# A transformer kernel of eleven phases on one core: one GpSimd addition for both rope halves, the high part of split states on ScalarE, and a new order of all four engines

## The chip, the cores and the metric

The kernel runs on one core of a Trainium2 chip. The metric is the device time of one execution in microseconds. Besides the timed runs there is one profiled execution, and every row below is from it. TensorE (PE) multiplies matrices and writes PSUM; VectorE (DVE), ScalarE (ACT) and GpSimd (POOL) work element by element; SyncE (SP) only issues transfers here. Each engine takes its own queue strictly in order, and semaphores tie the queues together.

## The reference

The input is `x` of 16 sequences, 256 tokens and 128 channels. Three sublayers follow each other:

```python
x = x + 0.5 * ffn(layernorm(x))
x = x + attention(layernorm(x))        # 16 heads of 8, causal, softmax
x = x + 0.5 * ffn(layernorm(x))
```

`ffn` is itself a transformer of two layers. A layer shifts half of the channels by one token, multiplies by `wqkv` (128 by 1536), divides the queries and keys of 8 heads of 64 by their length and scales them, applies rotary position factors, and attends over windows of 64 tokens with one window of look-back. It adds the output projection, normalises, and adds a gated MLP (`a * gelu(g)`, 341 hidden columns). The rotation is the part that matters here:

```python
def rotate_half(x):
    x1, x2 = jnp.split(x, 2, axis=-1)
    return jnp.concatenate([-x2, x1], axis=-1)
q = q * cos * scale + rotate_half(q) * sin * scale
```

## The kernel before

**Phases and steps.** Each of the 16 sequences goes through eleven phases (`PHASES`): dense phases 0, 2, 4, 6, 8, 10 and attention phases 1, 3, 7, 9 (local) and 5 (the full one). A phase is a list of steps, tuples of kind, sequence, phase and number, and a step is a list of parts, each on one engine (`PASSES`, `passes`). `("Q", s, ph, n)` is one block of 128 tokens of queries or keys with 512 columns; there are 4 for each sequence in each of the phases 0, 2, 6 and 8, that is 256. Its parts are three products on TensorE (L1702), squares on ScalarE (L1368), the product with the rope table on VectorE, which writes cosine and sine parts side by side (L1617, 128x1024), the sums of squares on VectorE (L1624), and two parts on GpSimd. `rope_join` adds the sine parts to the cosine parts with the halves of each head exchanged, by two instructions (L1228). `rope_scale` bounds the sums (L1235), raises them to the power -1/2 (L1238) and multiplies (L1242). Step `R` then turns the result on TensorE (L1934), and ScalarE copies it (L1386).

**The split.** TensorE multiplies in fp32r, so states are split in a high and a low part. `SPLIT` comes once for each sequence in phases 0, 2, 6 and 8 (64 in all). Both of its instructions run on VectorE: a cast of the state to `h_hi` (L1604), a wait of VectorE for itself, and the subtraction to `h_lo` (L1606). In phases 0 and 6 the state was set by ScalarE (step `STATE`, L1358 and L1359), in phases 2 and 8 by VectorE's addition after `W2` (L1575). The split after a normalisation (`LNT`) has its cast on ScalarE (L1364) and its subtraction on VectorE (L1611) already. Buffers `h_hi` and `h_lo` exist four times; before one is overwritten the engine waits on `bank_filled` for its last reader.

**The order.** Nothing in the code orders the engines by hand. While the kernel is built, `needs` lists what every part waits for, `due_dates` gives each part a due time out of the tables `START_AT`, `STRETCH`, `DUE`, `PHASE_DUE`, `LATER` and `NUDGE`, and `lay_out` plays the work through with the durations of `PASSES` and `passes`, `HANDOVER` between engines and the change of ScalarE's table. On each engine it takes the ready part that is due first, allowing for `PATIENCE`. Out come one in-order list for each of TensorE, ScalarE, VectorE and GpSimd, the buffer that each step uses, and `SERVED`, the order of SyncE's transfers. `tally` counts semaphore values along these lists.

```python
for step, part in POOL_ORDER:
    if (step, part) in POOL_NEEDS:
        pool.wait_ge(sems["prepared"], POOL_NEEDS[step, part])
    take(step, part)
```

## Time and profile before

| what | us |
|---|---|
| timed runs, median of three | 1718.89 |
| timed runs, lowest and highest | 1711.01, 1722.75 |
| the profiled execution | 1712.97 |
| its span (first to last instruction) | 1711.1 |

The span is what the rows divide; the profiled execution's own time is 1.9 us longer, which lies around the span. Busy time of an engine is the time in which it carried out instructions, and its idle time matters only where something later waits for it.

### The profile page before, as it was taken

The numbers are of one execution on the slowest core, as the hardware profiler recorded it, in microseconds if no ns is written. First come the engines' busy times: TensorE is split into PE (matmuls) and PEld (weight loads), VectorE is DVE, ScalarE is ACT, GpSimd is POOL, SyncE is SP. The second block draws the span as 40 slices with busy tenths as digits, with TensorE's granted clock in tenths as the row PEclk, the third lists the DMA queues.
The fourth block names the chain that finished last, engine by engine and source line by source line (L and its number), as shares of the span: only waits on it lengthen the run. The fifth ranks groups of instructions, "written<-read, shape, count | busy, mean of one in ns | idle before, by whom it ended". The sixth has DMA issues, their size and how long they took to land.

```text
span 1711.1 us, 48415 instructions
## 1 busy us (share of the span) xinstructions
PE 1513.9 (88%) x17754; PEld 1229.7 (72%) x17754; DVE 1459.9 (85%) x2978; ACT 1293.4 (76%) x3832; POOL 1310.2 (77%) x1546
## 2 busy tenths in 40 slices
PE   4788889889889999989989899999989899899987
PEld 3667677677767767767777777877766667678776
DVE  8788997888879879989888899988987979888885
ACT  2587768678867888778788877987875687787894
POOL 7899994557857988987889986989831779879890
PEclk9899999889989999999999999999999899999999
DMA  5101112110211101101010030001212002001000
GB/s 140 38 20 26 32 36 59 49 54 21 63 45 29 26 11 53 48 27 55 20 27 20 20 97 25 23 17 45 82 45 97 11 20 63 20 19 24 23 17 14
DMA packets 49635, 66.75 MB, mean 39 GB/s; under 512 B 8146, under 2 KB 32252, under 8 KB 49404
## 3 DMA queue, kind: packets, MB, share of 16 engines
q1 hardware_dynamic: 49404, 63.66, 13.8%
q8 instruction: 146, 2.39, 0.6%
q14 instruction: 85, 0.70, 0.1%
HBM read 22.75 MB, written 15.73 MB: 22 GB/s over the span
## 4 chain that ended last, share of the span: by engine, by line
POOL 31%; DVE 30%; PE 22%; ACT 9%; issue 8%; POOLq 0%; ACTq 0%; DVEq 0%
POOL sums L1238 11%; POOL parts L1228 8%; DVE parts L1617 7%; POOL parts L1242 7%; PE bank L1702 6%; ACT probs L1310 5%; DVE neg_full L1496 4%; DVE sums L1624 3%; DVE neg_max L1496 3%; POOL sums L1235 2%; PE bank L1752 2%; PE bank L1934 2%; PE bank L1889 2%; DVE probs L1526 2%; DVE normal L1563 2%
## 5 line engine op out<-in xcount | busy, mean ns | idle before, releaser
L1228 POOL TENSOR_TENSOR parts<-parts 128x256 f32<-128x256 f32 x512 | 388.7, 785 | 133.8 <-DVE parts L1617 132.5
L1238 POOL TENSOR_TENSOR sums<-sums,neg_half 128x8 f32<-128x8 f32 x256 | 434.8, 1699 | 21.3
L1310 ACT ACTIVATE probs<-bank,neg_max 128x128 f32<-128x128 f32 x1024 | 365.0, 415 | 65.5 <-DVE neg_max L1496 63.7
L1617 DVE TENSOR_TENSOR parts<-bank,rope 128x1024 f32<-128x1024 f32 x256 | 308.5, 1216 | 34.9 <-ACT squares L1368 33.2
L1242 POOL TENSOR_TENSOR parts<-parts,sums 128x512 f32<-128x512 f32 x256 | 282.3, 1103 | 37.9 <-POOL sums L1238 1.7
L1310 ACT ACTIVATION_READ_ACCUMULATOR probs<-bank,neg_max 128x1 f32 x1024 | 259.9, 255 | 0.0
L1934 PE MATMUL bank<-ident,parts 128*128 128x128 f32 x1024 | 165.2, 287 | 56.9 <-POOL parts L1242 50.6
L1368 ACT ACTIVATE squares<-bank 128x512 f32<-128x512 f32 x256 | 157.5, 625 | 52.1 <-PE bank L1702 29.9
L1702 PE MATMUL bank<-wqkv_hi,h_hi 128*128 128x512 f32 x384 | 182.0, 474 | 8.6 <-DVE h_lo L1606 5.0
L1934 PEld LDWEIGHTS bank<-ident,parts 128*128 128x128 f32 x1024 | 120.0, 145 | 91.6 <-issue 65.3
L1526 DVE TENSOR_TENSOR probs<-probs,prob_inv 128x1024 f32<-128x1024 f32 x128 | 174.2, 1361 | 4.4
L1800 PE MATMUL bank<-ident,probs 128*128 128x128 f32 x1024 | 147.6, 288 | 28.0 <-DVE probs L1526 13.2
L1496 DVE TENSOR_REDUCE neg_max<-bank 128x4 f32<-128x512 f32 x256 | 160.0, 680 | 11.6 <-PE bank L1773 10.5
L1624 DVE TENSOR_REDUCE sums<-squares 128x8 f32<-128x512 f32 x256 | 169.3, 674 | 0.2
L1339 ACT ACTIVATE turned<-bank 128x512 f32<-128x512 f32 x256 | 147.5, 652 | 23.6 <-PE bank L1800 23.1
L1800 PEld LDWEIGHTS bank<-ident,probs 128*128 128x128 f32 x1024 | 119.4, 147 | 52.5 <-issue 17.9
L1702 PE MATMUL bank<-wqkv_hi,h_lo 128*128 128x512 f32 x384 | 155.6, 405 | 0.0
L1702 PE MATMUL bank<-wqkv_lo,h_hi 128*128 128x512 f32 x384 | 155.2, 404 | 0.0
L1214 POOL TENSOR_SCALAR var_eps<-mean_var 128x2 f32<-128x2 f32 x112 | 29.7, 265 | 149.4 <-DVE mean_var L1556 144.3
L1773 PE MATMUL bank<-k_t,q_t 64*64 64x128 f32 (+1 forms) x4096 | 138.1, 260 | 0.0
L1496 DVE TENSOR_REDUCE neg_full<-bank 128x2 f32<-128x512 f32 (+1 forms) x192 | 119.7, 683 | 16.9 <-PE bank L1737 10.0
L1773 PEld LDWEIGHTS bank<-k_t,q_t 64*64 64x64 f32 x4096 | 127.5, 135 | 5.4 <-issue 0.6
(147 smaller groups left out, 3821.4 us busy)
## 6 DMA issues: line engine op xcount, KB each, us to landing
between<-val SPq DMA_DIRECT2D x192, 128.0 KB, 2.4
laid_dram<-halves SPq DMA_DIRECT2D x96, 128.0 KB
stacked_q<-laid_dram SPq DMA_DIRECT2D x16, 512.0 KB, 6.3
stacked_k<-laid_dram SPq DMA_DIRECT2D x16, 512.0 KB, 4.1
x_sb<-in_L_attn_x_dram SPq DMA_DIRECT2D x16, 128.0 KB, 2.5
out_dram<-x_sb SPq DMA_DIRECT2D x16, 128.0 KB, 1.8
laid_dram<-plain SPq DMA_DIRECT2D x8, 128.0 KB
raw_qkv<-in_L_ffn_wqkv_dram SPq DMA_DIRECT2D x3, 256.0 KB, 4.2
```

The costliest lines, as they stand in the source:

```text
L1228: last = nc.gpsimd.tensor_tensor(joined[:, :, dst], joined[:, :, dst], sines[:, :, src], ALU.add)
L1238: nc.gpsimd.tensor_tensor(sums[:, u], sums[:, u], neg_half[:], ALU.pow).then_inc(sems["pool_step"], 1)
L1242: nc.gpsimd.tensor_tensor(joined, joined, sums[:, u].rearrange("p (h o) -> p h o", o=1).to_broadcast([P, LOCAL_HEADS, LOCAL_D]), ALU.mult) ...
L1310: last = nc.scalar.activation(probs[:, u, block:block + wide].rearrange("p b j -> p (b j)"), bank[:, at:at + P * wide], ACT.Exp, bias=neg_ ...
L1496: nc.vector.tensor_reduce(dst, src, AX, ALU.max, negate=True).then_inc(sems["max_ready"], 1)
L1526: nc.vector.tensor_tensor(probs[:, u], probs[:, u], prob_inv[:, u].rearrange("p (r o) -> p r o", o=1).to_broadcast([P, BLOCKS, P]), ALU.mu ...
L1617: nc.vector.tensor_tensor(parts[:, u].rearrange("p o (h d) -> p o h d", d=LOCAL_D), bank[:].rearrange("p (o h d) -> p o h d", o=1, d=LOCAL ...
L1624: nc.vector.tensor_reduce(sums[:, ROPE_OF[step]], squares[:, SQUARES_OF[step]].rearrange("p (h d) -> p h d", d=LOCAL_D), AX, ALU.add).then ...
L1702: last = nc.tensor.matmul(dst, lhs, rhs, start=(n == 0), stop=(n == 2))
L1773: last = nc.tensor.matmul(bank[HALF * half:HALF * (half + 1), at + j0:at + P], q_t[a][rows, 2 * n + c, WINDOW * w:WINDOW * (w + 1)], k_t[a ...
L1800: last = nc.tensor.transpose(bank[:, P * n:P * (n + 1)], probs[:, u, block], ident[:])
L1934: last = nc.tensor.transpose(bank[:, P * c:P * (c + 1)], parts[:, u, 0, P * c:P * (c + 1)], ident[:])
```

## The change

`rope_join` becomes one instruction over 128x512. Both operands are seen as heads, halves and 32 columns, and the second one's halves are read in reversed order. The cast of `SPLIT` moves to ScalarE (a new function `split_state`); VectorE waits for it with `high_ready` in place of `vector_step`. The durations with which the order is planned are changed in some places, and the tables of due times (`START_AT` and those after it, here left out) are all new; `NUDGE` has 230 entries in place of 92. With them the order of all engines, the buffers and `SERVED` are new.

```diff
 PASSES = {
-    "SPLIT": [(DVE, 0.87)], "WO": [(PE, 1.65), (DVE, 0.88)],
+    "SPLIT": [(ACTE, 0.27), (DVE, 0.47)], "WO": [(PE, 1.65), (DVE, 0.88)],
...
-    "W1": [(PE, 0.74), (ACTE, 0.36), (DVE, 0.4)], "W2": [(PE, 1.3), (DVE, 1.01)], "OT": [(PE, 0.24), (ACTE, 0.28)], "WOF": [(PE, 0.45), (DVE, 0.36)],
-    "XB": [(POOL, 0.75)], "MT": [(DVE, 0.33), (PE, 0.5), (DVE, 0.6)], "Y": [(ACTE, 0.49)],
+    "W1": [(PE, 0.78), (ACTE, 0.36), (DVE, 0.4)], "W2": [(PE, 1.3), (DVE, 1.01)], "OT": [(PE, 0.24), (ACTE, 0.28)], "WOF": [(PE, 0.45), (DVE, 0.36)],
+    "XB": [(POOL, 0.75)], "MT": [(DVE, 0.45), (PE, 0.45), (DVE, 0.6)], "Y": [(ACTE, 0.49)],
...
-    "Q": [(PE, 0.79), (ACTE, 0.49), (DVE, 1.14), (DVE, 0.6), (POOL, 1.44), (POOL, 3.3)], "R": [(PE, 0.42), (ACTE, 0.49)],
-    "QF": [(PE, 0.85), (ACTE, 0.72), (DVE, 0.79)], "T": [(PE, 0.48), (ACTE, 0.49)]}
+    "Q": [(PE, 0.82), (ACTE, 0.49), (DVE, 1.14), (DVE, 0.6), (POOL, 1.25), (POOL, 3.35)], "R": [(PE, 0.4), (ACTE, 0.49)],
+    "QF": [(PE, 0.85), (ACTE, 0.72), (DVE, 0.79)], "T": [(PE, 0.46), (ACTE, 0.49)]}
...
     if kind in ("S", "E"):
-        return [(PE, 1.23 if not is_full(ph) else (0.88 if n else 1.25) if kind == "S" else (0.7 if n % 3 else 0.97))]
+        return [(PE, 1.1 if not is_full(ph) else (0.74 if n else 1.12) if kind == "S" else (0.7 if n % 3 else 0.97))]
...
     if kind == "N":
-        return [(DVE, 1.42)]
+        return [(DVE, 1.52)]
     if kind == "V":
-        return [(PE, 0.76), (ACTE, 0.28), (PE, 0.24), (DVE, 0.44)] if is_full(ph) else [(PE, 1.07), (ACTE, 0.5)]
+        return [(PE, 0.76), (ACTE, 0.28), (PE, 0.2), (DVE, 0.44)] if is_full(ph) else [(PE, 0.95), (ACTE, 0.5)]
...
-                joined = parts[:, u, 0].rearrange("p (h d) -> p h d", d=LOCAL_D)
-                sines = parts[:, u, 1].rearrange("p (h d) -> p h d", d=LOCAL_D)
-                hd = LOCAL_D // 2
-                for half in range(2):
-
-                    dst, src = slice(hd * half, hd * (half + 1)), slice(hd * (1 - half), hd * (2 - half))
-                    last = nc.gpsimd.tensor_tensor(joined[:, :, dst], joined[:, :, dst], sines[:, :, src], ALU.add)
-                last.then_inc(sems["rope_joined"], 1)
+                joined = parts[:, u, 0].rearrange("p (h o d) -> p h o d", o=2, d=LOCAL_D // 2)
+                sines = parts[:, u, 1].rearrange("p (h o d) -> p h o d", o=2, d=LOCAL_D // 2)
+                nc.gpsimd.tensor_tensor(joined, joined, sines[:, :, ::-1], ALU.add).then_inc(sems["rope_joined"], 1)
...
+            def split_state(step):
+
+                s, before = step[1], SPLIT_BEFORE[step]
+                whole = last_step({"STATE", "W2"}, step)
+                name = "state_set" if whole[0] == "STATE" else "state_ready"
+                act.wait_ge(sems[name], count(name, whole))
+                if before is not None:
+                    act.wait_ge(sems["bank_filled"], later("bank_filled", readers(before)))
+                nc.scalar.activation(h_hi[SPLIT_OF[step]][:], state[s][:, 0:T], ACT.Copy).then_inc(sems["high_ready"], 1)
...
                 elif kind == "SPLIT":
-                    if last_step({"STATE", "W2"}, step)[0] == "STATE":
-                        dve.wait_ge(sems["state_set"], count("state_set", last_step({"STATE"}, step)))
-                    else:
-                        dve.wait_ge(sems["state_ready"], count("state_ready", last_step({"W2"}, step)))
-                    before, h = SPLIT_BEFORE[step], SPLIT_OF[step]
-                    if before is not None:
-                        dve.wait_ge(sems["bank_filled"], later("bank_filled", readers(before)))
-                    nc.vector.tensor_copy(h_hi[h][:], state[s][:, 0:T]).then_inc(sems["vector_step"], 1)
-                    dve.wait_ge(sems["vector_step"], count("vector_step", step))
+                    dve.wait_ge(sems["high_ready"], count("high_ready", step))
+                    h = SPLIT_OF[step]
                     nc.vector.tensor_tensor(h_lo[h][:], state[s][:, 0:T], h_hi[h][:].bitcast(F32),
                                             ALU.subtract).then_inc(sems["split_ready"], 1)
```

## Rows read from the trace of the kernel before

**Rows 1.** The page: span and busy time of each engine (share, instructions):

```profile
span 1711.1 us, 48415 instructions
...
PE 1513.9 (88%) x17754; PEld 1229.7 (72%) x17754; DVE 1459.9 (85%) x2978; ACT 1293.4 (76%) x3832; POOL 1310.2 (77%) x1546
```

**Rows 2.** Windows: length, busy PE, PEld, DVE, ACT, POOL (instructions), clock, DMA share, GB/s:

```profile
100.00:1700.00 1600.00, 1443.62 (x17191) 1173.07 (x17187) 1377.12 (x2791) 1243.35 (x3694) 1229.28 (x1439) 0.97 0.14 37
...
945.00:972.00 27.00, 23.16 (x358) 19.29 (x358) 24.23 (x46) 23.26 (x81) 25.51 (x31) 1.00 0.09 22
```

**Rows 3.** The chain that ended last, whole span: by engine, then by line:

```profile
POOL 31%; DVE 30%; PE 22%; ACT 9%; issue 8%; POOLq 0%; ACTq 0%; DVEq 0%
...
by line: POOL sums L1238 10.6%; POOL parts L1228 8.3%; issue 7.8%; DVE parts L1617 7.2%; POOL parts L1242 6.9%; PE bank L1702 6.0%; ACT probs L1310 4.6%; DVE neg_full L1496 3.6%; DVE sums L1624 3.1%; DVE neg_max L1496 3.0%; POOL sums L1235 
```

**Rows 4.** Waits of TensorE: us, times, longest; last one group of instructions:

```profile
PE bank L1934 <- POOL parts L1242: 50.6, 54, 4.3
...
PE bank L1901 <- DVE normal L1563: 25.3, 17, 11.3
...
PE bank L1800 <- DVE probs L1526: 13.2, 20, 2.5
...
L1737 PEld LDWEIGHTS bank<-mask_full,ident_b 64*64 64x64 bf16 x384 | 7.7, 108 | 12.4 <-DMA stacked_k<-laid_dram 4.0 <-issue 3.9 <-DVE neg_full L1496 0.3
```

**Rows 5.** Groups of instructions: line, form, count, busy us, mean ns, idle before:

```profile
L1228 POOL TENSOR_TENSOR parts<-parts 128x256 f32<-128x256 f32 x512 | 388.7, 785 | 133.8 <-DVE parts L1617 132.5
```

**Rows 6.** One line's instructions: duration ns min/median/max:

```profile
L1228 POOL TENSOR_TENSOR parts<-parts x512: 708/732/1798, 23.4 to 1659.0; 128x256 f32<-128x256 f32 x171
...
L1242 POOL TENSOR_TENSOR parts<-parts,sums x256: 1041/1043/2085, 28.9 to 1665.9; 128x512 f32<-128x512 f32 x128
...
L1235 POOL TENSOR_SCALAR sums<-sums x256: 228/242/1231, 26.3 to 1662.8; 128x8 f32<-128x8 f32 x128
...
L1238 POOL TENSOR_TENSOR sums<-sums,neg_half x256: 1653/1656/2746, 27.1 to 1664.1; 128x8 f32<-128x8 f32 x128
...
L1606 DVE TENSOR_TENSOR h_lo<-state,h_hi x64: 424/426/1156, 18.3 to 1639.5; 128x256 fp32r<-128x256 f32 x64
...
L1611 DVE TENSOR_TENSOR h_lo<-bank,h_hi x80: 391/415/427, 72.7 to 1699.9; 128x256 fp32r<-128x256 f32 x80
```

**Rows 7.** Timeline, 181 to 192 us: start, length; first GpSimd, then VectorE:

```profile
185.25 2.57 POOL L1238 TENSOR_TENSOR sums<-sums,neg_half 128x8 f32<-128x8 f32 x1
...
188.96 2.40 POOL L1228 TENSOR_TENSOR parts<-parts 128x256 f32<-128x256 f32 x2
...
185.06 1.22 DVE L1526 TENSOR_TENSOR probs<-probs,prob_inv 128x1024 f32<-128x1024 f32 x1
...
189.36 1.40 DVE L1526 TENSOR_TENSOR probs<-probs,prob_inv 128x1024 f32<-128x1024 f32 x1
```

**Rows 8.** Groups of the split and of L1526; last two by duration min/median/max:

```profile
L1604 DVE CAST h_hi<-state 128x256 fp32r<-128x256 f32 x64 | 25.8, 403 | 2.3 <-PE bank L1702 1.3 <-ACT state L1359 0.3
...
L1606 DVE TENSOR_TENSOR h_lo<-state,h_hi 128x256 fp32r<-128x256 f32 x64 | 34.4, 538 | 2.2
...
L1526 DVE TENSOR_TENSOR probs<-probs,prob_inv 128x1024 f32<-128x1024 f32 x128 | 174.2, 1361 | 4.4
...
L1524 DVE RECIPROCAL prob_inv<-prob_sum 128x8 f32<-128x8 f32 x128 | 25.2, 197 | 32.5 <-ACT probs L1310 30.8
...
L1364 ACT ACTIVATE h_hi<-bank x80: 367/384/577, 72.2 to 1699.3; 128x256 fp32r<-128x256 f32 x80
...
L1526 DVE TENSOR_TENSOR probs<-probs,prob_inv x128: 1224/1226/2119, 53.0 to 1678.6; 128x1024 f32<-128x1024 f32 x128
```

**Rows 9.** The chain in order of time, 1684 to 1711 us: start, length, what:

```profile
1688.12 0.14 issue
...
1704.60 0.02 issue
```

**Rows 10.** Waits of ScalarE, the longest:

```profile
ACT probs L1310 <- DVE neg_max L1496: 63.7, 43, 3.2
```

More of the change, by code:

```diff
@@ L167 @@
[L167 to L170 removed]
[26 rows of a table removed]
[L197 to L202 removed]
[8 rows of a table removed]
[L211 removed]
[7 rows of a table removed]
+START_AT = (-146.9, -142.3, -458.8, -225.8, 39.3, 17.1, 149.3, 343.7, 1103.2, 1153.0, 855.1, 831.6, 1094.4, 946.4,
+            575.2, 1093.0)
@@ new lines @@
+STRETCH = 2.4717
+PATIENCE = (0.008, 0.0, 0.149, 0.697)
+DUE = {('E', 0, True): 24.6, ('FOLD', 0, False): 357.71, ('FOLD', 1, False): -179.97, ('LNH', 0, False): -125.77,
+       ('LNH', 1, False): -164.34, ('LNH', 2, False): -196.25, ('LNT', 0, False): 97.72, ('LNT', 1, False): 228.36,
+       ('LNT', 2, False): -32.48, ('LNX', 0, False): -99.02, ('LNX', 1, False): 271.99, ('MASKS', 0, False): 170.23,
[5 rows of a table added]
+       False): 2.3, ('SPLIT', 1, False): 16.47, ('STATE', 0, False): 687.9, ('STATE', 1, False): 353.42, ('T', 0,
+       False): -357.05, ('T', 1, False): -55.66, ('V', 0, False): 250.79, ('V', 0, True): -24.65, ('V', 1, False):
+       123.03, ('V', 1, True): 232.55, ('V', 2, True): -555.1, ('V', 3, True): -20.13, ('VAL', 0, False): 274.89,
+       ('VAL', 1, False): 633.81, ('VALF', 0, False): 355.59, ('VALF', 1, False): 857.28, ('W1', 0, False): 107.4,
[4 rows of a table added]
@@ new lines @@
+PHASE_DUE = {0: 192.38, 1: 2.46, 2: 173.79, 3: -404.42, 4: -66.84, 5: -104.61, 6: -5.63, 7: -56.17, 8: 224.03, 9:
+             -235.83, 10: 63.22}
+LATER = {(0, 0): 43.36, (0, 1): 578.39, (0, 2): 242.31, (0, 3): 614.64, (0, 4): 36.82, (0, 5): 285.3, (0, 6): 42.33,
[26 rows of a table added]
+NUDGE = {('E', 4, 5, 3): -8.39, ('E', 5, 5, 2): 2.84, ('E', 5, 5, 3): 1.02, ('E', 5, 5, 4): -6.73, ('E', 5, 5, 5):
+         -10.07, ('E', 6, 5, 2): -15.61, ('E', 8, 5, 0): -582.91, ('E', 8, 5, 3): -33.75, ('E', 12, 5, 1): -130.94,
+         ('E', 13, 5, 1): -52.12, ('E', 13, 5, 3): -142.92, ('E', 14, 5, 2): 7.18, ('E', 15, 5, 1): -66.92, ('E', 15,
+         5, 3): -65.73, ('E', 15, 5, 4): -64.1, ('LNH', 0, 2, 0): -159.5, ('LNH', 1, 2, 0): -203.36, ('LNH', 2, 4, 0):
+         309.01, ('LNH', 2, 8, 0): 486.11, ('LNH', 3, 2, 0): 410.81, ('LNH', 4, 10, 0): 379.39, ('LNH', 6, 10, 0):
+         795.7, ('LNH', 9, 10, 0): -622.56, ('LNH', 11, 4, 0): 386.0, ('LNH', 12, 2, 0): -675.3, ('LNH', 14, 4, 0):
+         551.52, ('LNT', 2, 10, 0): 252.15, ('LNT', 3, 4, 1): 455.1, ('LNT', 4, 2, 0): 283.63, ('LNT', 4, 4, 0):
+         19.05, ('LNT', 5, 2, 0): -430.37, ('LNT', 7, 8, 0): 230.96, ('LNT', 8, 4, 0): -429.31, ('LNT', 13, 2, 0):
+         -84.82, ('LNT', 13, 10, 0): 343.78, ('LNT', 14, 4, 1): 938.07, ('LNT', 15, 4, 0): 410.18, ('LNX', 3, 0, 0):
+         165.56, ('LNX', 10, 0, 0): -1127.88, ('LNX', 12, 0, 0): 6.57, ('LNX', 15, 0, 0): -264.71, ('MT', 3, 5, 0):
[22 rows of a table added]
+         -40.41, ('SPLIT', 6, 8, 0): -326.47, ('SPLIT', 10, 8, 0): 856.81, ('SPLIT', 13, 6, 0): -67.59, ('SPLIT', 14,
[6 rows of a table added]
+         9, 1): -223.99, ('VAL', 0, 8, 0): -105.47, ('VAL', 3, 8, 1): -345.91, ('VAL', 12, 2, 0): -194.96, ('VAL', 12,
+         2, 1): -198.42, ('VAL', 13, 0, 0): 253.78, ('VAL', 13, 0, 1): 248.62, ('VALF', 13, 4, 0): -402.87, ('W1', 1,
[14 rows of a table added]
@@ L838, in emits @@
         "STATE": [{}, {"state_set": 1}],
-        "SPLIT": [{"vector_step": 1, "split_ready": 1}],
+        "SPLIT": [{"high_ready": 1}, {"split_ready": 1}],
         "Q": [{}, {"squares_ready": 1}, {"rope_parts": 1}, {"squares_summed": 1}, {"rope_joined": 1},
@@ L1408, in _ @@
                     copy_heads(step)
+                elif step[0] == "SPLIT":
+                    split_state(step)
                 else:
```

17 lines of the change are left out of this document (removed), and 131 rows, old and new, of tables (DUE, LATER, NUDGE).

## The prediction

> **What bounds the kernel now.** I read the engine totals first. The span is 1711.1 us, and TensorE, VectorE, GpSimd and ScalarE are busy for 88, 85, 77 and 76% of it [rows 1]. No engine is full, and none is idle enough to be forgotten. Next comes the table by stretch. In the 1600 us between the start and the last steps TensorE is busy for 1443.6 us, so it idles for 156.4 us; where rope work lies thick (945 to 972 us) GpSimd is busy for 25.51 of 27 us [rows 2]. What a better order can win in the middle is therefore less than 156.4 us in the best case, since matmuls are neither added nor removed.
>
> Third is the chain that ended last. It runs 31% through GpSimd, 30% through VectorE, 22% through TensorE and 9% through ScalarE, and the join of the rope halves alone (L1228) is 8.3% of it [rows 3]. That is a list of engines taking turns, not one bottleneck. Last come the waits of TensorE. The largest is for the scaled rope parts, 50.6 us in 54 waits; those for VectorE (normal 25.3, probs 13.2) follow. Transfers hardly count: a TensorE weight load waited 4.0 us for one, so the new order of SyncE's queue (values shifted, halves written and spread, results stored) I price at nothing as long as that stays so [rows 4].
>
> **Part A, one join instead of two.** Removed are 512 GpSimd additions of 128x256 with a mean of 785 ns, or 1.57 us for each of 256 pairs [rows 5]; added are 256 additions of 128x512 in which the second operand's halves are read in reversed order. No row of before has that operation. From below: the 128x512 product with a broadcast operand, shortest 1.04 us. From above: the pair itself, 1.57 us, no gain; a loss I exclude from this term, since the same elements go in the same runs of 32 with one start fewer. Between these, a line through two undisturbed sizes: the 128x256 addition takes 0.73 us, and a one-operand 128x8 operation 0.24 us, which I take as the fixed part. So 256 columns cost 0.49 us and 512 columns 0.24 + 0.98 = 1.22 us [rows 6]. This is a plain addition with two full operands, so it lies nearer to this line than to the broadcast product.
>
> The means lie above the undisturbed times because GpSimd and VectorE get in each other's way. Two GpSimd additions from 188.96 us took 2.40 us instead of 1.43 while the VectorE product of two SBUF tensors (L1526) ran from 189.36 us. A power from 185.25 us took 2.57 us (its shortest is 1.653) beside the same product, begun at 185.06 us [rows 6, 7]. The pair carries 1.57 - 1.43 = 0.14 us of this. One start in place of two I let carry a bit over half, 0.09 us. The join then costs 1.22 + 0.09 = 1.31 us and saves 0.26 us, 66 us of GpSimd over 256. The new table of durations in the diff lowers its own entry for the join from 1.44 to 1.25, that is by 0.19 us, or 49 us over 256, which is the same size; I take 0.24 us, 61 us in all. On the chain stand 0.083 x 1711.1 = 142 us of L1228, or 142 / 1.57 = 90 pairs [rows 3, 5]; they give 90 x 0.24 = **22 us**. The bounds: nothing, and with the broadcast product's 1.04 plus 0.09 us, 90 x 0.44 = 40 us.
>
> **Part B, the cast on ScalarE.** 64 VectorE casts with a mean of 403 ns (25.8 us) go [rows 8]. VectorE has 0.30 x 1711 = 513 us of chain for 1460 us of work, 0.35 us for each us, so this gives 25.8 x 0.35 = 9 us [rows 1, 3]. ScalarE gets 64 copies of 128x256. Its copy of that size and type out of PSUM has a median of 384 ns [rows 8], so 24.6 us, and at 0.09 x 1711 / 1293 = 0.12 they cost 3 us. The same 0.38 us stands for a source in SBUF, for which there is no row of this form. Half of the splits (32) follow a VectorE addition to the state and so get a new crossing to ScalarE and back; crossings take 0.02 to 0.14 us on the chain [rows 9], which makes at most 32 x 0.28 = 9 us, times 0.35 some 2 us at middle values. Sum: **a gain of 4 us**. What hides the cast is ScalarE's own idle time. The new wait stands in ScalarE's in-order queue: behind it queue the exponentials, the copies of turned probabilities and the gelus, for which TensorE and VectorE wait. ScalarE's waits for row maxima are 63.7 us in 43, 1.48 us each [rows 10]. If every cast stopped it as long, 64 x 1.48 = 95 us at 0.12 would cost 11 us. Bounds of B: a gain of 9 us, a loss of 11 us.
>
> **Part C, the longer hold.** VectorE's subtraction of two SBUF tensors (L1606) has a shortest time of 424 ns and a longest of 1156: the difference of 732 ns is the length of one GpSimd addition. The same subtraction with one operand in PSUM (L1611) never took over 427 ns [rows 6, 8]. A longer GpSimd instruction so makes the two-SBUF operations wait longer. L1526 stands 135 ns above its shortest in the mean (1361 against 1226 in the median) and L1606 114 ns (538 - 424), in all 128 x 0.135 + 64 x 0.114 = 24.6 us [rows 8]. If all of it grew as 1.22 / 0.73, it would be 17 us more, 6 us on the chain. Only the waits behind joins grow, so I take **2 us lost**; bounds 0 and 6.
> By the Trainium skill (SBUF — State Buffer, section on the two separate sides) whichever of GpSimd and a VectorE instruction in a two-port mode or with two SBUF inputs begins first keeps the pair of ports for its whole instruction. The trace agrees for L1606 and L1526. By that rule one 1.22 us hold costs an operation that falls into it at random more than two of 0.73 us do (1.22 x 1.22 / 2 = 0.74 against 0.53 us squared), and a cast moved off VectorE ends one such clash; it would leave the sum as it is, since both stand in A to C.
>
> **Part D, the order laid out anew.** Nothing is computed that was not before; all four queues are sorted by other due times. The durations it plans with move by up to 0.14 us (a score unit 1.23 to 1.10, a weighted sum 1.07 to 0.95, the scaling of probabilities 1.42 to 1.52; the trace has 0.197 + 1.361 = 1.56 us for the last, so 1.52 is nearer [rows 8]). Without a new order I would count only half of A and B, because waits that ran beside the chain move onto it; that the order is made for the shorter steps is my reason for counting them whole. Beyond that, TensorE's two waits for VectorE above come to 38.5 us; I take some 15% of them, **6 us** [rows 4]. The bounds are wide: a third of the 156.4 us idle (52 us) won, or as much lost as the rope wait costs now (50.6 us).
>
> **The sum.** 22 + 4 - 2 + 6 = 30 us, from the profiled execution's 1712.97 us: 1683 us. The median of the three timed runs, 1718.89, is 5.9 us higher and their scatter is 11.7 us; I add half of that difference: **1686 us**, 1.9% below the median. Its own range is 1668 to 1702 us. The granted TensorE clock in the middle is 0.97 in the mean (the level of 2.4 GHz with short falls to 1.2) [rows 2]; I leave it there.
>
> **The rivals.**
> *Hidden* (0.20): the rope work is faster, but the chain's other strands, just as full, take its place, and the saved GpSimd time becomes GpSimd idle time. For: four engines within 12 points of one another. Against: 50.6 us of TensorE's waits are exactly for this work. Time: half of A and nothing else, 1719 - 11 = 1708 us, from 1702 to 1719.
> *Deeper* (0.14): the new order also fills a third of TensorE's idle 156.4 us. For: nothing in the rows forces these gaps to be there. Against: VectorE at 85% is itself close. Time: 1686 + 6 - 52 = 1640 at the far end, 1655 us as a middle.
> *The join costs what the pair cost* (0.05): GpSimd handles the reversed 4-dimensional pattern slower, and A is nought. Time: 1686 + 22 = 1708 us. For: no such pattern in the trace; against: the diff's 1.25 us.
> *Slower* (0.08): the new order brings TensorE's turning of the rope parts (L1934) nearer behind their scaling on GpSimd than before, and all that is queued behind it waits. Now this takes 50.6 us in 54 of 256 turnings. If twice as many wait, that is 50.6 us more against 30 won, 1719 + 20 = 1739 us. It decides from 50.6 + 30 = 81 us of such waits on. For: a plan made with mean durations leaves in-order queues no room for the 2.57 us powers. Against: the old order was of the same kind, and GpSimd now ends sooner.
>
> **Chances.** Forecast 0.53, hidden 0.20, deeper 0.14, join dear 0.05, slower 0.08. A measurement of this kernel can tell about 1% from no change, so 1701.7 us is the border for faster. Faster by over 1%: 0.53 + 0.14 = 0.67; within 1%: 0.20 + 0.05 = 0.25; slower by over 1%: 0.08. The range goes down to 1652 us, past the middle of the deeper case, and up to 1716 us, over most of the hidden one.
>
> **What will show each step.** A: 256 GpSimd instructions in place of 512, mean between 1.2 and 1.4 us, GpSimd busy near 1249 us. B: no VectorE cast of 128x256 but those of the weights, 64 more ScalarE copies of 0.38 us, VectorE near 1434 us busy, ScalarE near 1318. C: L1606's successor and L1526 with longest times of up to 1.22 us above their shortest, means up by no more than 0.1 us. D: TensorE's wait for the scaled rope parts below 40 us, and its idle middle near 130 us. Wrong would be: a join mean at or above 1.57 us; that wait above 81 us; waits of ScalarE for the state in tens of microseconds; or GpSimd's idle time grown by as much as its work fell, at an unchanged span.

## The result, and the profile after

| | before | after |
|---|---|---|
| median, us | 1714.93 (20 runs) | 1724.68 (20 runs) |
| lowest, highest | 1706.75, 1724.42 | 1714.97, 1734.62 |
| span of the profiled execution | 1711.1 | 1718.5 |

The ratio after to before is 1.0052, 95% interval 1.0034 to 1.007: a small loss of some 9 us where 1.9% of gain was forecast. 1686 us was wrong, and the time also lies above the range (1652 to 1716 us).

The page of after, engine totals, and below them the chain that ended last, by engine and by line:

```profile
span 1718.5 us, 48157 instructions
...
PE 1511.3 (88%) x17754; PEld 1223.7 (71%) x17754; DVE 1445.8 (84%) x2914; ACT 1325.7 (77%) x3904; POOL 1276.6 (74%) x1290
...
POOL 31%; PE 24%; DVE 21%; ACT 11%; issue 7%; DMA 4%; SPq 2%; POOLq 0%; ACTq 0%; DVEq 0%
```

Against [rows 1]: GpSimd is busy for 33.6 us less and VectorE for 14.1 us less. Yet GpSimd's idle time went from 1711.1 - 1310.2 = 400.9 to 1718.5 - 1276.6 = 441.9 us. The work went, and the engine waits instead. The chain holds as much of GpSimd as before (31%) [rows 3], and has 4% of DMA and 2% of SyncE's queue, which it did not have.

The windows of after, columns as in [rows 2]:

```profile
100.00:1700.00 1600.00, 1435.86 (x17076) 1162.86 (x17075) 1355.94 (x2715) 1269.66 (x3737) 1189.57 (x1188) 0.97 0.13 37
```

TensorE idles for 164.1 us in the middle where it idled for 156.4.

The changed operations of after, groups by line (busy us, mean ns, idle before), with the table loads of ScalarE:

```profile
L1257 POOL TENSOR_TENSOR parts<-parts 128x512 f32<-128x512 f32 x256 | 342.2, 1344 | 132.6 <-DVE parts L1650 131.7
...
L1566 DVE TENSOR_TENSOR probs<-probs,prob_inv 128x1024 f32<-128x1024 f32 x128 | 178.1, 1391 | 4.4
...
L1639 DVE TENSOR_TENSOR h_lo<-state,h_hi 128x256 fp32r<-128x256 f32 x64 | 39.4, 616 | 9.6 <-ACT h_hi L1389 9.3
...
L1389 ACT ACTIVATE h_hi<-state 128x256 fp32r<-128x256 f32 x64 | 27.5, 429 | 15.7 <-PE bank L1735 8.0 <-DVE state L1615 6.7
...
L1433 ACT ACT_TABLE_LOAD x48 | 61.6, 1283 | 0.9
...
L1338 ACT ACT_TABLE_LOAD x36 | 46.2, 1283 | 0.6
```

The join has its forecast size: 1.344 us, against 1.31. VectorE's products of two SBUF tensors got dearer in the mean: the scaling of probabilities 1391 ns after 1361, the subtraction 616 after 538 [rows 8]. ScalarE did the casts in 27.5 us; the last two groups and the 12 other loads make 96 table loads where before had these two:

```profile
L1395 ACT ACT_TABLE_LOAD x44 | 56.5, 1283 | 3.1 <-PE bank L1702 2.3
...
L1310 ACT ACT_TABLE_LOAD x31 | 39.8, 1283 | 0.6
```

and 13 others, 88 in all. The new order costs 8 x 1.283 = 10.3 us of ScalarE in table changes.

Waits of TensorE in after (us, times, longest):

```profile
PE bank L1967 <- POOL parts L1270: 56.9, 62, 4.2
PE bank L1934 <- DVE normal L1603: 23.2, 18, 11.3
...
PE bank L1833 <- DVE probs L1566: 19.4, 22, 3.2
```

Against [rows 4]: the wait for scaled rope parts grew from 50.6 to 56.9 us though GpSimd has less to do, the wait for scaled probabilities from 13.2 to 19.4 us, and a new one stands beside them, for the transfers of the full phase (the weight load's own wait, 4.0 us before):

```profile
PEld bank L1770 <- DMA stacked_k<-laid_dram: 11.8, 4, 5.4
...
PE bank L1770 <- DMA stacked_k<-laid_dram: 10.8, 4, 5.3
```

One place of the timeline of after shows what the engines do to each other (start, length):

```profile
708.27 1.28 POOL L1257 TENSOR_TENSOR parts<-parts 128x512 f32<-128x512 f32 x1 [0.61 <-DVE parts L1650]
...
708.34 2.30 DVE L1566 TENSOR_TENSOR probs<-probs,prob_inv 128x1024 f32<-128x1024 f32 x1
...
1264.08 1.23 DVE L1566 TENSOR_TENSOR probs<-probs,prob_inv 128x1024 f32<-128x1024 f32 x1
1264.12 2.32 POOL L1257 TENSOR_TENSOR parts<-parts 128x512 f32<-128x512 f32 x1
```

At 708 us the join began 0.07 us before the product; the join took its undisturbed 1.28 us and the product 2.30 instead of 1.22. At 1264 us the product began 0.04 us before the join; now the product is whole and the join takes 2.32 instead of 1.28. Which engine loses a little over 1 us (1.08 or 1.04) is decided by hundredths of a microsecond, and neither the order of before nor that of after looks at it. Below, *clash* means this.

### The profile page after: what moved, and what is told of

The parts are those of the page before. It is cut to its first block, busy times and chain, and to the rows that moved or that the text cites. A ratio compares the mean times of both kernels' runs of the same rounds, so it can differ in the third digit from the quotient of the medians.

```text
span 1718.5 us, 48157 instructions
## 1 busy us (share of the span) xinstructions
PE 1511.3 (88%) x17754; PEld 1223.7 (71%) x17754; DVE 1445.8 (84%) x2914; ACT 1325.7 (77%) x3904; POOL 1276.6 (74%) x1290
## 4 chain that ended last, share of the span: by engine, by line
POOL 31%; PE 24%; DVE 21%; ACT 11%; issue 7%; DMA 4%; SPq 2%; POOLq 0%; ACTq 0%; DVEq 0%
POOL sums L1266 11%; POOL parts L1270 7%; POOL parts L1257 7%; PE bank L1735 6%; DVE parts L1650 5%; ACT probs L1338 4%; DMA laid_dram<-halves 3%; DVE neg_full L1536 3%; POOL sums L1263 2%; PE bank L1967 2%; PE bank L1922 2%; PE bank L1833 2%; DVE sums L1657 2%; POOL rstd L1249 2%; PE bank L1785 2%
## 5 line engine op out<-in xcount | busy, mean ns | idle before, releaser
L1266 POOL TENSOR_TENSOR sums<-sums,neg_half 128x8 f32<-128x8 f32 x256 | 438.2, 1712 | 21.3
L1257 POOL TENSOR_TENSOR parts<-parts 128x512 f32<-128x512 f32 x256 | 342.2, 1344 | 132.6 <-DVE parts L1650 131.7
L1967 PE MATMUL bank<-ident,parts 128*128 128x128 f32 x1024 | 164.0, 284 | 64.5 <-POOL parts L1270 56.9
L1566 DVE TENSOR_TENSOR probs<-probs,prob_inv 128x1024 f32<-128x1024 f32 x128 | 178.1, 1391 | 4.4
L1833 PE MATMUL bank<-ident,probs 128*128 128x128 f32 x1024 | 152.0, 291 | 31.7 <-DVE probs L1566 19.4
L1247 POOL TENSOR_SCALAR var_eps<-mean_var 128x2 f32<-128x2 f32 x112 | 33.8, 302 | 172.9 <-DVE mean_var L1596 167.4
L1922 PE MATMUL bank<-q_t,wo 128*128 128x256 f32 x512 | 125.7, 389 | 9.8 <-ACT q_t L1378 6.0
```

What stands on the lines that cost most here:

```text
L1257: nc.gpsimd.tensor_tensor(joined, joined, sines[:, :, ::-1], ALU.add).then_inc(sems["rope_joined"], 1)
L1266: nc.gpsimd.tensor_tensor(sums[:, u], sums[:, u], neg_half[:], ALU.pow).then_inc(sems["pool_step"], 1)
L1566: nc.vector.tensor_tensor(probs[:, u], probs[:, u], prob_inv[:, u].rearrange("p (r o) -> p r o", o=1).to_broadcast([P, BLOCKS, P]), ALU.mu ...
L1833: last = nc.tensor.transpose(bank[:, P * n:P * (n + 1)], probs[:, u, block], ident[:])
L1922: last = nc.tensor.matmul(bank[:, 0:T], w[:, c], o[:, c], start=(c == 0), stop=(c == CHUNKS - 1))
L1967: last = nc.tensor.transpose(bank[:, P * c:P * (c + 1)], parts[:, u, 0, P * c:P * (c + 1)], ident[:])
```

## The experiments

Every ratio is to runs of before, which were repeated beside each batch of kernels on the same chip; the table gathers them.

| run | operations | order of the queues | ratio | 95% |
|---|---|---|---|---|
| after | both edits | after's | 1.0052 | 1.0034 to 1.007 |
| old_join | join | before's | 0.9992 | 0.9973 to 1.001 |
| old_cast | cast | before's | 1.0011 | 0.9995 to 1.0028 |
| old_both | both edits | before's | 1.0008 | 0.9989 to 1.0026 |
| new_two | cast | after's | 1.0165 | 1.0143 to 1.0187 |
| new_dve | join | after's | 1.0157 | 1.0136 to 1.0178 |
| new_none | neither | after's | 1.0174 | 1.0149 to 1.0198 |
| old_spread | neither, no wait for laid halves | before's | 0.9991 | 0.9977 to 1.0005 |
| new_spread | both, no wait for laid halves | after's | 1.004 | 1.0025 to 1.0055 |
| after_exclusive | both edits | after's, moved with the exclusion | 0.9715 | 0.9693 to 0.9737 |
| after_ignorant | both edits | after's, moved without it | 0.9909 | 0.9886 to 0.9932 |
| before_exclusive | neither | before's, moved with it | 0.9737 | 0.9715 to 0.976 |
| both_exclusive | both edits | before's, moved with it | 0.9601 | 0.9578 to 0.9624 |
| both_ex_two | cast | that of both_exclusive | 0.9784 | 0.9732 to 0.9835 |
| sh_before_1 | neither | before's, 300 blind moves | 1.0047 | 1.002 to 1.0073 |
| sh_before_2 | neither | before's, 300 others | 1.0068 | 1.0042 to 1.0094 |
| sh_after_1 | both edits | after's, 300 blind moves | 1.0081 | 1.0059 to 1.0104 |

**The edits in the order of before.** Three kernels of before: with the one addition, with the cast on ScalarE (put into its queue where the plan has the state ready; after's `split_state` and `high_ready`), and with both.

```diff
-                for half in range(2):
...
-                    last = nc.gpsimd.tensor_tensor(joined[:, :, dst], joined[:, :, dst], sines[:, :, src], ALU.add)
-                last.then_inc(sems["rope_joined"], 1)
+                nc.gpsimd.tensor_tensor(joined, joined, sines[:, :, ::-1], ALU.add).then_inc(sems["rope_joined"], 1)
```

```diff
+        at = [n for n, y in enumerate(queue) if (y in DONE_AT and y[0][0] != "SPLIT" and
+                                                 DONE_AT[y] - passes(y[0])[y[1]][1] >= ready)][0]
+        queue.insert(at, (x, 0))
```

Expected of old_join:

> The kernel of before with its order, buffers and due times untouched; only the two GpSimd additions of rope_join become one. Theory G (the edits gain, the new order gives it back): the chain holds 90 pairs, each now shorter by 1.57 - 1.34 = 0.23 us, so up to 21 us less than before; with parallel strands taking over half, 10 us; ratio 0.988 to 0.994. Theory H (the edits are hidden behind other strands): within 3 us of before, ratio 0.998 to 1.002, and GpSimd's idle time grows by what its work loses, some 50 us.

Expected of old_cast:

> The order of before; only the cast of each split state moves to ScalarE, put into its queue at the time at which the plan of before has the state ready. Theory G: 4 us faster (9 us off VectorE's share of the chain, 5 us back on ScalarE and for crossings), ratio 0.995 to 1. Theory H: nothing, ratio 0.999 to 1.002. Theory L (the cast costs on ScalarE, because the in-order queue stops there for the state): 5 to 11 us slower, ratio 1.003 to 1.006, with ScalarE waits for the state above 30 us.

Expected of old_both:

> The order of before with both edits. Theory G: the sum of the two single runs, 14 to 25 us faster than before, ratio 0.985 to 0.992; the new order would then have to cost 24 to 35 us. Theory H: ratio 0.998 to 1.002, and the new order costs the 9 us that after is slower.

Measured: 0.9992, 1.0011, 1.0008. In a fixed order the edits are worth nothing that can be told from no change, together or alone. The engine totals of old_join, its scaling of probabilities, and two waits of TensorE:

```profile
span 1711.8 us, 48159 instructions
...
PE 1509.6 (88%) x17754; PEld 1225.0 (72%) x17754; DVE 1472.9 (86%) x2978; ACT 1294.7 (76%) x3832; POOL 1270.5 (74%) x1290
```

```profile
L1521 DVE TENSOR_TENSOR probs<-probs,prob_inv 128x1024 f32<-128x1024 f32 x128 | 180.5, 1410 | 4.4
```

```profile
PE bank L1929 <- POOL parts L1237: 41.9, 43, 3.6
...
PE bank L1795 <- DVE probs L1521: 23.1, 31, 3.6
```

GpSimd is busy for 39.7 us less and idle for 40.4 us more, at an unchanged span: what the prediction gave as the mark of a hidden gain. The waits show where it went. TensorE's wait for rope parts fell by 8.7 us (50.6 to 41.9), and its wait for scaled probabilities rose by 9.9 us (13.2 to 23.1) [rows 4]. A product that falls behind a join can now be held by an instruction of 1.28 us and not of 0.73; its mean rose from 1361 to 1410 ns [rows 8], and VectorE is busy for 13.0 us more. So the gain was not only hidden, it was handed from one pair of engines to the other. The trace of old_both has the same trade (42.6 and 21.7 us of the two waits); that the two sums cancel at the end of the chain is read from the unchanged time and was not tested apart.

**The edits undone in the order of after.** Three kernels of after: with two additions per join, with the cast on VectorE, with both undone.

```diff
                 elif step[0] == "SPLIT":
-                    split_state(step)
+                    pass
...
-                    dve.wait_ge(sems["high_ready"], count("high_ready", step))
...
+                    nc.vector.tensor_copy(h_hi[h][:], state[s][:, 0:T]).then_inc(sems["vector_step"], 1)
+                    dve.wait_ge(sems["vector_step"], count("vector_step", step))
```

Expected of new_none:

> The order and the due times of after, but with two GpSimd additions for each join and the cast on VectorE directly ahead of its subtraction: the new order alone. Theory G: the order costs 24 to 35 us on top of undone edits worth 14 to 25 us less: 1.015 to 1.025 of before. Theory H: 9 us slower than before like after itself, ratio 1.003 to 1.008. Either way TensorE waits for the spread transfers of the full phase should show as in after, some 22 us of matmuls and weight loads, where before had 4.

Expected of new_two:

> After with two GpSimd additions for each join; its order and the cast on ScalarE stay. The new order without both edits stood at 1.0174 of before, after itself at 1.0052, so the edits together are worth 1.2% there. If the join carries it (theory P: the new order leaves the rope work on GpSimd no room): ratio 1.013 to 1.017. If the cast carries it (theory Q): 1.005 to 1.009. If both alike: 1.011.

Expected of new_dve:

> After with the cast on VectorE directly ahead of its subtraction; one addition for the join. Theory P: ratio 1.005 to 1.008, the cast is worth little. Theory Q: 1.013 to 1.017. If both alike: 1.011.

Measured: 1.0174, 1.0165, 1.0157. Undoing the join costs 1.1% (1.0165 against 1.0052), undoing the cast 1.05%, and both together 1.2%, not their sum. The same edits were worth nothing in the order of before. They have no price of their own, then. The departures are not alike: shorter work put into the order of before changed nothing, the old and longer work put back into the order of after cost about 1%, whichever part of it came back. The reading is that an order loses when a step outlasts the time that it was planned with and wins nothing when a step ends early; these six kernels fit it, and no run tests it apart. The 1.0174 of new_none lies where theory G had it, though old_both (1.0008 against 0.985 to 0.992) had refuted G; and of the theories for new_two and new_dve none had each edit costing as much as both. TensorE's wait for rope parts in new_two:

```profile
PE bank L1972 <- POOL parts L1275: 85.0, 83, 4.2
```

That is 28.1 us above after's 56.9, of which 18.5 us reach the median (1743.17 against 1724.68).

**The new wait for transfers.** Can the loss of after be its four waits for the full phase's stacked keys? In both orders the rearranged halves were loaded from a constant tensor and not from the one that the halves are written to, directly behind the writes, so that SyncE waits for no write ahead of them. The full phases then compute with the constants of that tensor in place of the halves.

```diff
-                    sp.wait_ge(written[u][w], WRITES * nth)
...
-                                 laid[u, w].rearrange("j b (d c) t -> (j b d) (c t)", c=CHUNKS)).then_inc(spread[u], 16)
+                                 ready_made[w].rearrange("j b (d c) t -> (j b d) (c t)", c=CHUNKS)).then_inc(spread[u], 16)
```

Expected of new_spread:

> After, but the spread stacks of the full attention are loaded from an array that was filled once at the start, directly behind the writes of the halves and with no wait for them (so the full attention computes with constants in place of its queries and keys; the writes stay, the order of all engines stays). The stacks should land some 8 us after the halves are ready, not 15 to 17. Theory D (the new order plans the first score steps too close behind these transfers, and that is what makes it slower): TensorE's waits for stacked_k, 10.8 us in matmuls and 11.8 in weight loads, vanish, and the time falls by 8 to 12 us, to 0.998 to 1.001 of before. Theory E (other work would have filled or repeated these waits): a fall by 0 to 3 us, 1.003 to 1.006.

Expected of old_spread:

> The same edit in before (constants for queries and keys of the full attention, no wait for the writes). Its weight loads waited 4.0 us for these transfers. Theory D: 2 to 4 us faster, ratio 0.997 to 0.999. Theory E: ratio 1.

Measured: 1.004 for after's order and 0.9991 for before's. The first is 0.12% or 2 us below after's 1.0052, with intervals that overlap. But the edit ended only a third of the waits:

```profile
PEld bank L1773 <- DMA stacked_k<-ready_dram: 8.1, 3, 4.8
...
PE bank L1773 <- DMA stacked_k<-ready_dram: 7.2, 2, 4.7
```

Of the 11.8 and 10.8 us of after, 8.1 and 7.2 us remained. What the run shows is that 3.7 us less of such waits for weight loads and 3.6 us less for products bring at most a few microseconds; what the rest costs stays open, and with it whether the transfers carry part of the loss.

**Is it the clash?** The theory now: what the order is worth is set by which GpSimd instruction lies beside which VectorE product. It was put to the test by moving steps in the four queues, a few places at a time. A search played the queues through with durations taken from the traces and kept each move that ended earlier. In after_exclusive, before_exclusive and both_exclusive a GpSimd instruction and a VectorE operation with two SBUF inputs could not run at once: the later one waited for the end of the first. In after_ignorant, the control, the same search ran without that rule. Nothing else is changed; the moves stand in the kernel as offsets:

```diff
+def shifted_order(order, shifts):
+
+    steps = [int(x) for run in shifts.split() for x in [run.split("*")[0]] * int((run + "*1").split("*")[1])]
...
+    return [order[n + x] for n, x in enumerate(steps)]
+PE_ORDER, ACT_ORDER, DVE_ORDER, POOL_ORDER = (shifted_order(x, y) for x, y in zip((PE_ORDER, ACT_ORDER, DVE_ORDER, POOL_ORDER), SHIFTS))
```

Expected of after_exclusive:

> After with the same instructions, buffers and transfers; only the four queues are changed, by steps moved a few places past steps of other sequences. The moves were chosen by playing the queues through with the occupancies that the traces of before and after show for each kind of step, and with one rule more than the planner in the kernel has: a GpSimd instruction on SBUF data and a VectorE one with two SBUF operands (L1566, L1639 of after) exclude each other for their whole length. Theory C (these clashes are what the planner does not know and what decides the worth of an order): well faster than after and than before, ratio 0.955 to 0.975. Theory V (the chip's own scatter of durations eats any plan): 0.99 to 1.005.

Expected of after_ignorant:

> The control of after_exclusive: the same start, the same kind and number of tries, the same occupancies, but without the rule that the two exclude each other. Theory C: it gains clearly less, since its plan counts on overlaps that do not take place: ratio 0.98 to 0.995, at least 1.5% slower than after_exclusive. Theory V: the same as after_exclusive within 0.5%.

Expected of before_exclusive:

> The same search with the rule, starting from before and with the operations of before (two additions for a join, cast on VectorE). Theory C: 0.960 to 0.980, and slower than the kernels with both edits in orders found the same way by 6 to 15 us, which would be the edits' worth where the order is fitted to them. If the edits are worth nothing even then: the same as after_exclusive within 3 us.

Expected of both_exclusive:

> The same search with the rule and both edits, but starting from the order of before (old_both). If the start does not matter, within 0.5% of after_exclusive, which clears the new due times themselves of being worse ground; Theory C: 0.955 to 0.975.

Measured: 0.9715, 0.9909, 0.9737, 0.9601. With the same operations and the same starting order, the search that knew the clash won 3.4% on after and the one that did not 1.4%. The engine totals and the product's and join's groups of after_exclusive:

```profile
span 1669.0 us, 48157 instructions
...
PE 1513.7 (91%) x17754; PEld 1220.0 (73%) x17754; DVE 1430.4 (86%) x2914; ACT 1314.2 (79%) x3904; POOL 1257.9 (75%) x1290
```

```profile
L1366 POOL TENSOR_TENSOR parts<-parts 128x512 f32<-128x512 f32 x256 | 333.9, 1310 | 124.2 <-DVE parts L1759 122.9
...
L1675 DVE TENSOR_TENSOR probs<-probs,prob_inv 128x1024 f32<-128x1024 f32 x128 | 165.2, 1291 | 4.4
```

and the same two groups of after_ignorant (span 1703.4 us):

```profile
L1365 POOL TENSOR_TENSOR parts<-parts 128x512 f32<-128x512 f32 x256 | 345.0, 1355 | 138.3 <-DVE parts L1758 137.4
...
L1674 DVE TENSOR_TENSOR probs<-probs,prob_inv 128x1024 f32<-128x1024 f32 x128 | 173.4, 1355 | 4.4
```

The product came down by 100 ns (1391 to 1291) where the exclusion was known and by 36 ns where it was not; the join by 34 ns, against a rise of 11. VectorE is busy for 15.4 us less than in after and GpSimd for 18.7, though they do the same work, and TensorE's wait for rope parts fell from 56.9 to 37.1 us. In after_ignorant the two engines together are busy for 5.4 us less than in after, and the wait stands at 59.9. Fewer clashes go with the larger gain, as the theory wants; that they are its only cause is not shown. The two searches also came to other orders elsewhere, and each is one outcome of a search. How much such outcomes scatter is seen from both_exclusive: the same instructions and the same rule, only another start, and it is 1.1% faster than after_exclusive (1651.05 against 1669.44 us), where 0.5% at most was expected. The 1.9% between after_exclusive and after_ignorant is more than that, but not by much.

The fastest kernel, both_exclusive: totals, product, and TensorE's wait:

```profile
span 1644.6 us, 48161 instructions
...
PE 1495.0 (91%) x17754; PEld 1208.2 (73%) x17754; DVE 1420.8 (86%) x2914; ACT 1304.6 (79%) x3898; POOL 1248.2 (76%) x1290
```

```profile
L1659 DVE TENSOR_TENSOR probs<-probs,prob_inv 128x1024 f32<-128x1024 f32 x128 | 161.7, 1264 | 4.4
```

```profile
PE bank L2060 <- POOL parts L1363: 35.0, 47, 4.0
...
PE bank L1926 <- DVE probs L1659: 9.9, 19, 1.3
```

The product is 40 ns above its shortest, 1224, where after had 167. What are the two edits worth when each side has an order fitted in the same way? From the order of before the search came to 1672.54 us without them (before_exclusive) and to 1651.05 with them: 21.5 us or 1.3%, in one and the same batch. From the order of after it came to 1669.44 us with them, and that is only 3.1 us below before_exclusive. So the two comparisons say 21.5 and 3.1 us, and one found order from each start can't tell which is nearer.

**What does the join do in a fitted order?** The fastest kernel with two additions again, same queues; and for the question whether the order of before was a lucky draw, orders disturbed by 300 small moves, each neutral by the durations alone.

Expected of both_ex_two:

> The fastest kernel so far (both edits, queues laid with the exclusion, 0.960 of before), with the join undone: two additions of 128x256 in place of one of 128x512, same queues. If the join is worth its busy time where the order is made for it: 0.965 to 0.972, a loss of 8 to 20 us. If it is worth as little as in the order of before: 0.960 to 0.963.

Expected of sh_before_1:

> The instructions of before; 300 small moves of neighbouring steps of different sequences in the four queues, each neutral by the durations alone, without looking at which GpSimd instruction stands beside which VectorE product. Theory (the order of before is well fitted by luck to the exclusion of GpSimd and VectorE, and blind moves lose that): 1.003 to 1.008 of before. Rival (it is no special draw): within 0.2% of before, or better.

Expected of sh_before_2:

> As the first shuffled order of before, with other random moves. Theory of the favourable draw: again 1.003 to 1.008, so both lose. Rival: one above and one below 1, or both within 0.2%.

Expected of sh_after_1:

> The instructions of after; 300 small blind moves in its four queues. If the order of after is fitted to its own clashes as well, it loses as those of before do: 1.009 to 1.013 of before. If it is an ordinary draw: 1.003 to 1.007, as the kernel after has it (1.005).

Measured: 0.9784, against 0.9601 with the join: a loss of 1.8%, more than the 0.965 to 0.972 expected. The totals of both_ex_two and its wait:

```profile
span 1685.2 us, 48417 instructions
...
PE 1515.4 (90%) x17754; PEld 1224.0 (73%) x17754; DVE 1425.1 (85%) x2914; ACT 1309.0 (78%) x3898; POOL 1290.6 (77%) x1546
```

```profile
PE bank L2065 <- POOL parts L1368: 55.7, 60, 4.5
```

GpSimd's busy time rose by 42.4 us and the median by 29.5 (1651.05 to 1680.59, in two batches), where in the order of before 39.7 us of the same work were worth nothing. The spans shown differ by more, 40.6 us, because the profiled execution of both_exclusive was its fastest of five and that of both_ex_two its slowest of four. Between these two, TensorE's wait for rope parts differs by 20.7 us (35.0 to 55.7) and TensorE's own busy time by 20.4 us (1495.0 to 1515.4), at a granted clock of 0.977 and 0.963. Over all their executions the clock stood at 0.970 to 0.978 in both_exclusive and at 0.963 to 0.970 in both_ex_two. As with the edits undone in after, the loss holds the price of an order that no longer fits as well as that of the work.

The disturbed orders gave 1.0047 and 1.0068 for before and 1.0081 for after. For before both lose, and both intervals lie above 1: its order is fitted too, and 300 moves that are free by durations alone cost it 8 to 12 us. The two sizes lie in the expected 1.003 to 1.008, but the reason given there, lost luck with the clashes, is not borne out. The totals of sh_before_2, its product and its wait:

```profile
PE 1513.2 (88%) x17754; PEld 1225.4 (71%) x17754; DVE 1459.3 (85%) x2978; ACT 1293.6 (75%) x3832; POOL 1311.0 (76%) x1546
...
L1564 DVE TENSOR_TENSOR probs<-probs,prob_inv 128x1024 f32<-128x1024 f32 x128 | 172.3, 1346 | 4.4
...
PE bank L1972 <- POOL parts L1280: 58.6, 68, 4.3
```

VectorE and GpSimd are as busy as in before to within 1 us each, and the product is 15 ns shorter in the mean, so it clashes no more than before does; TensorE's wait for rope parts grew all the same, from 50.6 to 58.6 us. An order can lose 0.7% without more clashes. Of after's, whose interval (1.0059 to 1.0104) overlaps that of after itself, the run does not tell the two cases apart.

## Why the prediction was wrong, by its own steps

**What bounds the kernel.** Right as far as it went: no engine is the bottleneck, and the chain takes turns. It named the clash in part C, and left it out of its picture of what sets the order's worth.

**A, the join.** The size of the operation was right: 1.344 us against 1.31 forecast, in 256 instructions. The pair was taken too dear. 2 x 785 ns counts the overlap of the two in the record twice; by busy time a pair occupied 388.7 / 256 = 1.518 us and the join occupies 342.2 / 256 = 1.337, so 0.18 us are saved and not 0.24, 46.5 us in all and not 61. GpSimd's total fell by only 33.6 because its other groups took 12.9 us longer, though their work is the same. Of the 22 us on the chain nothing arrived in the order of before (0.9992), with the trade of waits shown above.

**B, the cast.** The 25.8 us left VectorE, and ScalarE's copies took 0.429 us in the mean, not 0.38. The new wait for the state was no disaster: 6.7 us for VectorE's state and 8.0 us for products of TensorE in after, and 9.3 us of VectorE's waiting for the cast ahead of the subtraction. The 0.02 to 0.14 us that the prediction took for crossings are rows of issue time and show no crossing to ScalarE and back. The gain of 4 us was not there; in the order of before the cast alone measures 1.0011, whose interval reaches from a gain of 0.9 to a loss of 4.8 us.

**C, the longer hold.** The mechanism was right, and the longest times fit. One reading on the way was not: the subtraction's longest time, 732 ns above its shortest, is not one GpSimd addition. In before it fell behind a scaling of rope parts (L1242, 1.04 us) that had begun 0.17 us earlier, and behind an addition of 0.73 us no subtraction lost more than 0.44 us:

```profile
919.48 1.04 POOL L1242 TENSOR_TENSOR parts<-parts,sums 128x512 f32<-128x512 f32 x1
...
919.65 1.16 DVE L1606 TENSOR_TENSOR h_lo<-state,h_hi 128x256 fp32r<-128x256 f32 x1
```

Durations in after, min/median/max, of the join, the scaling of probabilities and the subtraction:

```profile
L1257 POOL TENSOR_TENSOR parts<-parts x256: 1261/1282/2318, 18.4 to 1673.6; 128x512 f32<-128x512 f32 x128
```

```profile
L1566 DVE TENSOR_TENSOR probs<-probs,prob_inv x128: 1224/1225/2350, 60.2 to 1692.4; 128x1024 f32<-128x1024 f32 x128
```

```profile
L1639 DVE TENSOR_TENSOR h_lo<-state,h_hi x64: 393/424/1541, 13.2 to 1651.3; 128x256 fp32r<-128x256 f32 x64
```

The excess is now 1.13 and 1.15 us, under the 1.22 forecast as the most; the means rose by 30 and 78 ns, under 0.1 us. The size was off: 2 us lost. In the order of before the mean rose by 49 ns, 6.3 us on VectorE, and TensorE's wait for it by 9.9 us, above the upper bound of 6. A mean spread over all instructions, priced with VectorE's share of the chain, can undercount a delay that strikes just before TensorE wants the result.

**D, the new order: the step that failed.** "That the order is made for the shorter steps is my reason for counting them whole", with 6 us on top. The runs part the terms. In a fixed order A to C were worth 0.08% of loss (interval 0.11% of gain to 0.26% of loss) and not 24 us; the new order on top of them cost 1.0052 / 1.0008, 0.44% or 7.5 us, instead of giving 6. The reason was a fair one and only half true: the order of after does fit the shorter steps (undone, they cost over 1%), but as a whole it is no better an order than that of before. What it lacks is in part known: it lays GpSimd and VectorE side by side as if they did not meet, and moved with that rule it gains 3.4%. The order of before lacks the same and gains 2.6% by it, so this is something a better order can use and does not tell why after is the worse of the two; VectorE and GpSimd together are busy for 3.7 us more in after than in old_both.
By the rule of the Trainium skill (SBUF — State Buffer, section on the two separate sides) the engine of the two that begins later is fully blocked until the first one's instruction ends. The places at 708 and 1264 us come near it: a full block would have cost the later one 1.21 and 1.19 us, and it lost 1.08 and 1.04. For powers the traces say otherwise, as the last section shows. I had used the clash for the price of one delay and not for the value of an order.
Of the marks I gave, TensorE's rope wait should have been below 40 us and was 56.9, its idle middle near 130 and was 164.1, GpSimd 1249 and was 1276.6, VectorE 1434 and was 1445.8, ScalarE 1318 and was 1325.7, in which the 10.3 us of table changes are. The transfers that I priced at nothing became 22.6 us of TensorE's waits (weight loads and products, in part at the same time); of their price it is known only that ending a third of them changed the time by 2 us, within the noise.

**The rivals.** *Hidden* described the edits exactly, in the order of before: GpSimd's idle time grew by what its work fell. *Slower* had the right sign for after and the wrong size and place: its wait stood at 56.9 us, not 101, and decides from 81. That the *join costs what the pair cost* is ruled out by its 1.344 us. The time that *deeper* gave (1655) is in reach: both_exclusive took 1651.05, but by an order that the change does not have. With fitted orders the two edits gave 21.5 us in one pair, close to the 24 that the sum had for A to C, and 3.1 us in the other. So the sum may be near what the edits can give or far above it; it was wrong in that the order of after would collect it.

**What stays open.** Why exactly the order of after is 0.44% worse than that of before: 3.7 us more of VectorE's and GpSimd's time, 8 more table changes and the transfers all point that way; only the last were touched by a run, and that ended a third of their waits. What the edits are worth in fitted orders, 3 us or 21, is open too. Whether the orders found are near the best was not tried.

## What to carry to other kernels

In a kernel whose engines take turns at 75 to 90%, the value of a shorter operation can't be read from its share of the chain: measure it in the old order, and with orders fitted to each side by the same means, several for each side (here two fitted orders of the same instructions were 1.1% apart, and the edits' worth was 3 or 21 us by which of them was taken), for a kernel that is undone in the new order's queues mixes the edit's price with the order's fit. When a planner lays out GpSimd and VectorE, let it know that a GpSimd addition or scaling over hundreds of columns and a VectorE operation with two SBUF inputs exclude each other, while a running power holds no such VectorE operation up; here re-laying with that rule, applied to all GpSimd instructions, gave 2.6% on before and 3.4% on after with the same instructions, and without it 1.4% on after, with one found order for each figure. Take what an engine saves from busy time divided by count and not from the mean duration, where records of neighbours overlap.

## What was not expected of the hardware

The granted clock of TensorE was 0.970 to 0.978 in the five executions of both_exclusive, and 0.957 to 0.964 in the twelve of old_both. TensorE's busy time went from 1513.5 to 1495.0 us with it, between the two profiled executions. So a part of the fastest kernel's gain seems to have come through the clock. A gain does not need it: after_exclusive, 2.85% faster than before, stood at 0.964 to 0.966. Before_exclusive, with four of its five executions at 0.968 to 0.972, shows that not only the fastest order has it. What in the order decides it was not tested.

A power of GpSimd (L1266, 1.65 us) does not hold VectorE up, although it is GpSimd's longest instruction. Of the 128 products of two SBUF tensors in after, 36 began while a power ran, some with over 1.5 us of it left, and none took more than 4 ns above the shortest; of the 64 subtractions 18 did, and none took more than 33 ns above. Behind joins and scalings the same operations lost up to 1.15 us. Before has the same: 42 products began during a power and lost 30 ns at most. One such place in after:

```profile
673.15 1.66 POOL L1266 TENSOR_TENSOR sums<-sums,neg_half 128x8 f32<-128x8 f32 x1
...
673.29 1.23 DVE L1566 TENSOR_TENSOR probs<-probs,prob_inv 128x1024 f32<-128x1024 f32 x1
```

The other way round it is held: the power from 185.25 us [rows 7], begun 0.19 us after a product, took 2.57 us. In after the longest stands 2710 - 1653 = 1057 ns above the shortest:

```profile
L1266 POOL TENSOR_TENSOR sums<-sums,neg_half x256: 1653/1656/2710, 22.3 to 1675.2; 128x8 f32<-128x8 f32 x128
```

So a plan that lets a running power exclude VectorE for its whole length, as the searches here did, is too strict. A search without that was not tried.
